# What a row gather of GpSimd waits for: its own view of the third last landing, or SyncE's count of the fourth last

## The chip, the cores and the metric

One Trainium2 chip (trn2), one of its NeuronCores. The metric is the device time of one execution in microseconds (us). The kernel before took 2842.06 us, the median of three runs (2833.11 to 2845.28).

## The reference

A relational graph layer and a mixture-of-experts layer, all float32, on N = 6250 nodes with 256 features.

```python
w_full = einsum('rb,bdo->rdo', w_comp, weight)        # 16 relations from 8 bases
msg = (feat @ w_full)[etypes, src] * norm             # 200,000 edges, sorted by dst
agg = segment_sum(msg, dst, num_segments=N)
x = x + relu(agg + h_bias + feat @ loop_weight)       # feat = layernorm(x)
# then: top 2 of 16 experts (256 -> 512 -> 256) for every node, added, and a layer norm
```

The targets `dst` are drawn as 6250·u² with u uniform, so low nodes have many edges and high nodes few. The host turns the order of the nodes round: the kernel begins with the nodes that have few edges.

## The kernel before, in words

The edges lie in 1568 blocks of 128. For each block GpSimd gathers the 128 source rows (1 KB each, 128 KB in all) from `feat` by an indirect DMA (line 1069) into `rows`, a ring of RB = 56 blocks. The nodes are cut into windows of 16. A step is one block with one window: VectorE builds the matrix `S` that spreads the block's edges over 16 nodes and 8 bases (lines 1141 to 1150), and TensorE multiplies it with the gathered rows into `psW` (line 1278, two passes of a float32 product). There are 1960 steps, 7 to a turn, 280 turns: each step moves on by a block or by a window, so a stretch of nodes with few edges has more steps to a block. After each 16 windows (a tile) ScalarE takes the sums out of `psW` (lines 1338, 1340), and TensorE transposes them and multiplies them with the basis weights (lines 1231, 1244).

What orders the gathers:

- **The lists.** `blocks(i)` of GpSimd issues 112 gathers in 8 groups of 14; there are 14 such passes, the first and the last written out with constants, those between in a loop whose waits take computed values. Before each group GpSimd waits until TensorE has finished the turns that read the ring's places (`s_P`, line 1059), and copies the next 14 columns of indices (line 1045).
- **The pacing.** Before each gather, `landed` (lines 1047 to 1050) waits for an earlier one: the gather of block j waits until that of block j - AHEAD has landed. A gather raises one of ROWS = 8 semaphores by 16 on landing, in turn, so GpSimd waits on that block's own semaphore. `ahead` (lines 719 to 722) does the same for the first 28 blocks, which are gathered at the end of the stage before (`expand`).
- **The count.** SyncE does little in this stage but wait for the landings one after the other, in order, and raise `s_in` by one for each (lines 1023 to 1026). TensorE waits on this one count before each turn (line 1275). Four times SyncE also waits for a turn of VectorE and loads the next coefficients (about 1 MB, lines 1032 and 1033). Before its first count it issues the loads of the layer's weights (lines 1018 to 1022).

When the graph layer ends, the experts' stage begins behind a barrier, then the last stage that adds up and normalizes.

Of the kernel before, what the change touches and what calls it, by code (L numbers as in the profile page):

```python
# [78 lines left out]
RB = 56  # L79
GB = 14  # L80
ROWS = 8
AHEAD = 3
IB = 2 * (RB // GB)
EG = 2
CTL_PART = (84, 72, 64, 60)
assert NBLK % RB == 0 and RB % GB == 0 and RB % ROWS == 0 and AHEAD < ROWS and sum(CTL_PART) == TURNS and all(n % NS == 0 for n in CTL_PART)
assert all(t + n <= 8 * i <= TURNS for t, n, i in CHUNK)
# [12 lines left out]
def at_least_one(e, loaded, held):  # L100

    for to, of in zip(held, loaded):
        e.reg_alu(to, of, 1, ALU.max)
    return held
# [74 lines left out]
def later(i):  # L179

    return not isinstance(i, int) or i > 0
# [468 lines left out]
def expand(nc, d, wcd, halfs, win_n, ident, tables, wend, pairs, jcol, wcol, spread, dstS, wgtS, coefS, s_got, s_feat, srcT, idx, rows, s_row):  # L650
# [5 lines left out]
    with ctx:  # L656
# [57 lines left out]
        def _(e):  # L714
# [4 lines left out]
            def ahead(j):  # L719
                if j >= AHEAD:  # L720
                    e.wait_ge(s_row[(j - AHEAD) % ROWS], 16 * ((j - AHEAD) // ROWS + 1))
                e.indirect_dma_start(rows[:, j * H:(j + 1) * H], None, d.feat, bass.IndirectOffsetOnAxis(ap=idx[:, j:j + 1], axis=0)).then_inc(s_row[j % ROWS], 16)
# [245 lines left out]
def graph_layer(nc, d, a, ctl, pairs, room, wend, srcT, dstS, wgtS, coefS, ident, wb, lw, hb, gw, s_w, logit, choice, mean, rstd, idx, rows, s_row):  # L968
# [5 lines left out]
    with ctx:  # L974
# [3 lines left out]
        def sem(name):  # L978
            return ctx.enter_context(nc.semaphore(name))
# [22 lines left out]
        s_in = sem("rows_in")  # L1002
# [10 lines left out]
        @blk.sync  # L1013
        def _(e):


            for c in range(HC):
                e.dma_start(wb[:, c, :, :], a["L0_gnn_weight"].rearrange("b (c p) o -> c p b o", p=P)[c, :, :, :]).then_inc(s_w, 16)
            e.dma_start(lw[:, :, :], a["L0_gnn_loop_weight"].rearrange("(c p) o -> p c o", p=P)).then_inc(s_w, 16)
            e.dma_start(hb[:, :], a["L0_gnn_h_bias"].partition_broadcast(P)).then_inc(s_w, 16)  # L1020
            e.dma_start(choice[0][:, :], a["L0_ffn_gate_b"].partition_broadcast(P)).then_inc(s_gb, 16)
            e.dma_start(gw[:, :, :], a["L0_ffn_gate_w"].rearrange("(c p) e -> p c e", p=P)).then_inc(s_w, 16)
            def rows_in(i):
                for j in range(RB):
                    e.wait_ge(s_row[j % ROWS], i * (RB // ROWS * 16) + (j // ROWS + 1) * 16)
                    e.sem_inc(s_in, 1)  # L1026
            i0 = 0
            for k, (t, n, i1) in enumerate(CHUNK):
                with e.Fori(i0, i1) as i:
                    rows_in(i)  # L1030
                e.wait_ge(s_S, t + n)
                c = slice(t * U * B, (t + n) * U * B)
                e.dma_start(coefS[:, c], d.coef[:, c]).then_inc(s_late[k], 16)
                i0 = i1
            with e.Fori(i0, NBLK // RB) as i:
                rows_in(i)

        @blk.gpsimd
        def _(e):
            ch = Chain(e, s_pool)  # L1040
            regs, room_held = ([e.alloc_register(f"{n}{q}") for q in range(IB)] for n in ("room", "room_held"))
            last = NBLK // (IB * GB) - 1

            def list_in(group, q):
                ch.add(e.tensor_copy(idx[:, q * GB:(q + 1) * GB], srcT[:, bass.ds(group * GB, GB)]))

            def landed(i, n):

                e.wait_ge(s_row[n % ROWS], i * (IB * GB // ROWS * 16) + (n // ROWS + 1) * 16)
                e.sem_inc(s_paced, 1)  # L1050

            def blocks(i):
                e.load(regs, room[0:1, bass.ds(i * IB, IB)])
                free = at_least_one(e, regs, room_held)
                for q in range(0 if later(i) else EG, IB):
                    if later(i) or q >= RB // GB:

                        e.wait_ge(s_P, free[q])
                        e.sem_inc(s_turn, 1)
                    if later(i) or q > EG:  # L1060
                        ch.wait()
                    if q < IB - 1 or not isinstance(i, int) or i < last:
                        list_in(i * IB + q + 1, (q + 1) % IB)
                    else:
                        e.sem_inc(s_turn, 1)
                    for u in range(GB):
                        at = (q * GB + u) % RB
                        landed(i, q * GB + u - AHEAD)
                        e.indirect_dma_start(rows[:, at * H:(at + 1) * H], None, d.feat, bass.IndirectOffsetOnAxis(ap=idx[:, q * GB + u:q * GB + u + 1], axis=0)).then_inc(s_row[at % ROWS], 16)  # L1069
            e.iota(choice[1][:, :], [[1, X]], base=-X, channel_multiplier=0, allow_small_or_imprecise_dtypes=True).then_inc(s_xno, 1)  # L1070
            e.iota(node.rearrange("p (m n) -> p m n", m=2), [[1, 2], [2, WIN // 2]], base=0, channel_multiplier=0, allow_small_or_imprecise_dtypes=True).then_inc(s_node, 1)
            blocks(0)
            with e.Fori(1, last) as i:
                ch.base, ch.n = IB * i - EG, 0
                blocks(i)
            ch.base, ch.n = IB * last - EG, 0
            blocks(last)
# [995 lines left out]
```

## Time and profile before

| | |
|---|---|
| median of 3 runs | 2842.06 us (2833.11 to 2845.28) |
| the profiled execution's own time, and its span | 2844.61 us, 2842.7 us |
| mean granted TensorE clock | 0.914 of full speed |
| busy: TensorE, VectorE, ScalarE, GpSimd | 78%, 34%, 23%, 64% |
| gathers of the graph layer (line 1069) | 1540, first start 159.5 us, last 2199.5 us |

The profile's page gives busy time by engine and line; the trace can be asked what an engine waited for before an instruction (its releaser), for a stretch of time, and for the instructions in order of time. In the rows "PE" is TensorE's matmuls, "POOL" GpSimd, "SPq" SyncE's queue; "x80" is a count; "us" of an idle time are summed over the count, and "issue" is idle time for which no releaser is seen. An indirect DMA's "busy" is the time in which GpSimd makes it, not its transfer.

### The profile page before, as it was taken

What the parts mean: (1) busy time and instruction counts of PE and PEld (TensorE: products, weight loads), DVE (VectorE), ACT (ScalarE), POOL (GpSimd) and SP (SyncE); (2) the same over time, 40 slices, a digit from 0 to 9 for tenths busy, and PEclk for the clock granted to TensorE, in tenths of its full rate; (3) what the DMA queues carried; (4) which work ended last, traced back from release to release, by engine and by line L of the source; (5) the groups of instructions that cost most, each with busy time, mean ns of one, the idle gap of its engine ahead of it and who ended that gap; (6) DMA issues with size and microseconds to landing.
All of it is one profiled execution on the core that took longest, in us unless ns stands there. A gap on an engine that the chain in (4) does not pass through costs nothing. (4 is left out here: it accounts for less than half of the span.)

```text
span 2842.7 us, 43421 instructions
## 1 busy us (share of the span) xinstructions
PE 2224.4 (78%) x11549; PEld 1849.9 (65%) x11550; DVE 967.4 (34%) x2172; ACT 654.3 (23%) x1539; POOL 1815.4 (64%) x2000
## 2 busy tenths in 40 slices
PE   1779999999988888876776768557655579999987
PEld 0567787877776666664664646445444379999975
DVE  6733333342332322222222212112112453333347
ACT  2522323232222211111110101001000233333345
POOL 0557777777777777777777777777777035555544
PEclk9999999999999989998898878789777799999998
DMA  6544444344333434334333333333333552222246
GB/s 210 160 146 119 121 118 123 116 120 134 116 117 111 129 111 116 111 112 122 109 109 109 118 107 108 108 100 114 103 103 94 187 182 70 70 70 70 70 131 220
DMA packets 146270, 338.66 MB, mean 119 GB/s; under 512 B 36674, under 2 KB 56290, under 8 KB 146051
## 3 DMA queue, kind: packets, MB, share of 16 engines
q0 software_dynamic: 89296, 245.33, 29.5%
q1 hardware_dynamic: 39311, 59.54, 6.1%
q10 hardware_dynamic: 17588, 32.88, 3.5%
q8 instruction: 36, 0.59, 0.1%
q14 instruction: 39, 0.32, 0.0%
HBM read 292.84 MB, written 47.97 MB: 120 GB/s over the span
## 5 line engine op out<-in xcount | busy, mean ns | idle before, releaser
L1069 POOL DMA_INDIRECT rows<-feat,idx x1540 | 1468.1, 953 | 548.9 <-issue 462.5
L1278 PE MATMUL psW<-rows,S 128*128 x3920 | 1065.1, 433 | 413.8 <-SPq L1026 380.8
L1278 PEld LDWEIGHTS psW<-rows,S 128*128 128x128 f32 x3920 | 842.1, 219 | 632.7 <-issue 495.0
L1150 DVE TENSOR_TENSOR S<-psHere,coefS 128x896 f32<-128x896 f32 x280 | 301.6, 1090 | 1379.0 <-PE psW L1278 1372.4
L1338 ACT COPY z<-psW 128x512 f32<-128x512 f32 x196 | 114.9, 586 | 1461.3 <-PE psW L1278 1460.6
L1244 PE MATMUL psG<-wb,zT 128*128 128x256 f32 (+1 forms) x1600 | 353.5, 379 | 0.0
L1244 PEld LDWEIGHTS psG<-wb,zT 128*128 128x128 f32 (+1 forms) x1600 | 300.6, 188 | 44.7
L1729 PE MATMUL psH<-xT,w1x 128*128 128x128 f32 x1840 | 226.8, 277 | 0.3
L1680 POOL DMA_INDIRECT expert_rows<-os,at_rows x114 | 114.0, 1000 | 171.3 <-DVE os L1788 171.3
L1729 PEld LDWEIGHTS psH<-xT,w1x 128*128 128x128 f32 x1840 | 216.5, 193 | 2.0 <-issue 1.9
L1738 PE MATMUL psO<-w2s,hT 128*128 x912 | 215.7, 379 | 0.0
L1702 ACT ACTIVATE hT<-psH,b1T 128x128 f32<-128x128 f32 x460 | 131.5, 368 | 315.6 <-PE psH L1729 315.6
L1676 POOL DMA_INDIRECT xs<-y_rows,at_rows x116 | 115.0, 991 | 100.7 <-POOLq L1408 56.6
L1738 PEld LDWEIGHTS psO<-w2s,hT 128*128 128x128 f32 x912 | 164.6, 190 | 17.6
L1788 DVE TENSOR_TENSOR os<-psO,b_b 128x256 f32<-128x256 f32 x114 | 48.4, 425 | 236.9 <-PE psO L1738 236.4
L1231 PE MATMUL psZ<-ident,z 128*128 128x128 f32 x784 | 113.8, 283 | 13.5 <-ACT zT L1352 8.8
L1340 ACT COPY psW<-zero 128x512 f32<-128x512 f32 x196 | 115.6, 590 | 6.2
L1352 ACT COPY zT<-psZ 128x512 f32<-128x512 f32 x196 | 108.1, 589 | 18.4 <-PE psZ L1231 18.4
L1231 PEld LDWEIGHTS psZ<-ident,z 128*128 128x128 f32 x784 | 83.7, 141 | 36.1 <-ACT zT L1352 20.1
L1772 DVE COPY w1x<-w1s 128x1024 f32 x116 | 86.1, 742 | 0.0
L1898 PE MATMUL psSum<-g,dg 128*128 128x256 f32 x200 | 56.0, 405 | 17.3 <-DMA g<-expert_rows 17.1
L1141 DVE TENSOR_TENSOR psHere<-dstS,psHere 128x224 f32<-128x224 f32 (+1 forms) x140 | 55.3, 395 | 31.5 <-DVE S L1150 25.1
(284 smaller groups left out, 1442.1 us busy)
## 6 DMA issues: line engine op xcount, KB each, us to landing
rows<-feat,idx POOLq DMA_INDIRECT x1568
g<-expert_rows SPq DMA_DIRECT2D x24, 512.0 KB, 5.5
w1s<-in_L_ffn_w SPq DMA_DIRECT2D x8, 1024.0 KB, 10.0
w2s<-in_L_ffn_w SPq DMA_DIRECT2D x16, 512.0 KB, 10.1
feat<-rows SPq DMA_DIRECT2D x24, 256.0 KB, 3.0
fts<-feat ACTq DMA_DIRECT2D x24, 256.0 KB, 2.8
h<-in_x ACTq DMA_DIRECT2D x24, 256.0 KB
y_rows<-y ACTq DMA_DIRECT2D x24, 256.0 KB
```

What stands on the lines that cost most here:

```text
L1069: e.indirect_dma_start(rows[:, at * H:(at + 1) * H], None, d.feat, bass.IndirectOffsetOnAxis(ap=idx[:, q * GB + u:q * GB + u + 1], axis=0) ...
L1150: e.tensor_tensor(S[h0 + h][:, :].rearrange("p (s b n) -> p s b n", s=U, b=B), both[:, h * U:(h + 1) * U, :].unsqueeze(2).to_broadcast([P, ...
L1231: last = e.transpose(to[:, k * P:(k + 1) * P], z[:, w * H + c * P:w * H + (c + 1) * P], ident[:, :])
L1244: last = e.matmul(psG[0:Q, m * H:(m + 1) * H], zT[:, at:at + Q], wb[:, c, b, :], start=False, stop=(c == HC - 1 and b == B - 1))
L1278: last = e.matmul(psW[:, bass.ds(bank[u], H)], S[h][:, u * ZC:(u + 1) * ZC], rows[:, bass.ds(slot[u], H)], start=False, stop=True, skip_gr ...
L1338: e.copy(z[:, 2 * k * H:2 * (k + 1) * H], bank).then_inc(s_z, 1)
L1340: e.copy(bank.rearrange("p (w o) -> p w o", w=2), zero[:, :].unsqueeze(1).to_broadcast([P, 2, H])).then_inc(s_clear, 1)
L1676: e.indirect_dma_start(xs[n % XS][:, :], None, d.y, bass.IndirectOffsetOnAxis(ap=at_rows[:, n, 0:1], axis=0)).then_inc(s_in[n % XS], 16)
L1680: e.indirect_dma_start(d.two, bass.IndirectOffsetOnAxis(ap=at_rows[:, n + 4, 1:2], axis=0), os_[n % 2][:, :], None).then_inc(s_out[n % 2], 16)
L1702: last = e.activation(hT[k][:, c * P:(c + 1) * P], psH[k][:, c * P:(c + 1) * P], ACT.Relu, bias=b1T[:, bass.ds(ex * FC + c, 1)])
L1729: last = e.matmul(psH[k][:, f * P:(f + 1) * P], w1x[k][:, c * F + f * P:c * F + (f + 1) * P], xT[k][:, c * P:(c + 1) * P], start=(c == 0), ...
L1738: last = e.matmul(psO[k][:, 0:H], hT[k][:, c * P:(c + 1) * P], w2s[:, bass.ds(ex, 1), c, :].rearrange("p e f -> p (e f)"), start=(c == 0), ...
```

## The change

Two places differ. `landed` waits on `s_in`, the count that SyncE keeps, and no longer on the semaphore of the block's own gather; and AHEAD is 4, in `landed` and in `ahead`.

```diff
@@ -79,7 +79,7 @@
 ROWS = 8
-AHEAD = 3
+AHEAD = 4
 IB = 2 * (RB // GB)
@@ -1046,7 +1046,7 @@
             def landed(i, n):
 
-                e.wait_ge(s_row[n % ROWS], i * (IB * GB // ROWS * 16) + (n // ROWS + 1) * 16)
+                e.wait_ge(s_in, i * (IB * GB) + (n + 1))
                 e.sem_inc(s_paced, 1)
```

In the order of GpSimd's instructions this shows in the loop of `blocks`. First the head of the loop, a group's first gathers, before (line 1059's wait is named turn_done, line 1026's count rows_in):

```order
 L1045 COPY idx<-srcT 128x14
 L1049 REGISTER_ALU
 L1069 DMA rows<-feat,idx 128x256 [waits row5]
 L1069 DMA rows<-feat,idx 128x256 [waits row6]
 L1069 DMA rows<-feat,idx 128x256 [waits row7]
 L1049 REGISTER_ALU
 L1069 DMA rows<-feat,idx 128x256 [waits row0]
```

The same place with the change:

```order
 L1045 COPY idx<-srcT 128x14
 L1049 REGISTER_ALU
 L1069 DMA rows<-feat,idx 128x256 [waits rows_in]
 L1049 REGISTER_ALU
 L1069 DMA rows<-feat,idx 128x256 [waits rows_in]
 L1049 REGISTER_ALU
 L1069 DMA rows<-feat,idx 128x256 [waits rows_in]
```

The value waited for differs for every gather now, so nearly every one has a register operation ahead of it: 110 to a pass of the loop against 15, where 8 gathers shared one value. No other engine's instructions move.

## Rows read from the trace of the kernel before

**Rows 1.** The page: busy by line; line, engine, operation | busy, mean ns | idle before, releaser
```profile
L1069 POOL DMA_INDIRECT rows<-feat,idx x1540 | 1468.1, 953 | 548.9 <-issue 462.5
L1278 PE MATMUL psW<-rows,S 128*128 x3920 | 1065.1, 433 | 413.8 <-SPq L1026 380.8
```
**Rows 2.** Waits of the whole span: who waited for whom: us in total, times, longest us
```profile
POOL rows L1069 <- issue: 462.5, 1422, 3.4
PE psW L1278 <- SPq L1026: 380.8, 132, 7.8
POOL rows L1069 <- DMA rows<-feat,idx: 85.6, 116, 4.6
```
**Rows 3.** GpSimd in order of time, 1471 to 1486 us: start, us, what [idle before]
```profile
1469.73 1.48 POOL L1069 DMA_INDIRECT rows<-feat,idx  x1 [0.64 <-DMA rows<-feat,idx]
1471.52 0.95 POOL L1069 DMA_INDIRECT rows<-feat,idx  x1 [0.30 <-issue]
1472.77 0.95 POOL L1069 DMA_INDIRECT rows<-feat,idx  x1 [0.30 <-issue]
1474.02 0.95 POOL L1069 DMA_INDIRECT rows<-feat,idx  x1 [0.30 <-issue]
1475.27 0.98 POOL L1069 DMA_INDIRECT rows<-feat,idx  x1 [0.30 <-issue]
...
1482.81 0.94 POOL L1069 DMA_INDIRECT rows<-feat,idx  x1 [0.30 <-issue]
1484.06 0.94 POOL L1069 DMA_INDIRECT rows<-feat,idx  x1 [0.30 <-issue]
```
**Rows 4.** The stage's end, 2195 to 2210 us, in order of time
```profile
2199.46 0.95 POOL L1069 DMA_INDIRECT rows<-feat,idx  x1 [0.89 <-DMA rows<-feat,idx]
2203.64 4.97 PE L1278 MATMUL psW<-rows,S 128*128 x14 [2.50 <-SPq L1026]
```
**Rows 5.** Waits, 560 to 2200 us
```profile
POOL rows L1069 <- issue: 377.6, 1160, 3.4
PE psW L1278 <- SPq L1026: 369.8, 121, 7.8
POOL rows L1069 <- DMA rows<-feat,idx: 58.7, 80, 3.3
```
**Rows 6.** GpSimd at the longest waits for a landing, one near each load of coefficients
```profile
655.61 0.95 POOL L1069 DMA_INDIRECT rows<-feat,idx  x1 [3.30 <-DMA rows<-feat,idx]
954.81 0.95 POOL L1069 DMA_INDIRECT rows<-feat,idx  x1 [2.96 <-DMA rows<-feat,idx]
1328.10 0.94 POOL L1069 DMA_INDIRECT rows<-feat,idx  x1 [2.28 <-DMA rows<-feat,idx]
1622.62 0.94 POOL L1069 DMA_INDIRECT rows<-feat,idx  x1 [1.91 <-DMA rows<-feat,idx]
```
**Rows 7.** GpSimd, 311 to 316 us: one of 14 long waits without a releaser
```profile
311.68 0.98 POOL L1069 DMA_INDIRECT rows<-feat,idx  x1 [0.16 <-issue]
315.28 0.95 POOL L1069 DMA_INDIRECT rows<-feat,idx  x1 [2.62 <-issue]
```
**Rows 8.** The stage's start: GpSimd's gathers, SyncE's loads and first count
```profile
159.49 1.00 POOL L1069 DMA_INDIRECT rows<-feat,idx  x1 [0.57 <-issue]
167.61 0.95 POOL L1069 DMA_INDIRECT rows<-feat,idx  x1 [4.61 <-DMA rows<-feat,idx]
163.46 0.49 SPq L1022 DMA_DIRECT2D gw<-in_L_ffn_gate_w  x1
L1026 SPq EVENT_SEMAPHORE  x1568: 17/17/17, 164.2 to 2203.3; - x196
```
**Rows 9.** Busy by stretch: us, PE busy (x), PEld, DVE, ACT, POOL, clock, DMA, GB/s
```profile
260.00:360.00 100.00, 93.71 (x462) 78.49 (x460) 33.19 (x79) 31.06 (x56) 71.67 (x81) 1.00 0.40 119
560.00:2200.00 1640.00, 1219.88 (x4995) 981.77 (x4994) 432.69 (x873) 243.16 (x438) 1201.11 (x1329) 0.88 0.38 112
```
**Rows 10.** Waits, 360 to 560 us
```profile
POOL rows L1069 <- DMA rows<-feat,idx: 8.4, 15, 1.2
PE psW L1278 <- SPq L1026: 1.4, 4, 0.6
```
**Rows 11.** All engines at 367 to 369 us: a turn's end and the list behind it
```profile
367.88 1.09 DVE L1150 TENSOR_TENSOR S<-psHere,coefS 128x896 f32<-128x896 f32 x1 [25.68 <-PE psW L1278]
368.33 0.21 POOL L1045 COPY idx<-srcT 128x14 int32 x1
```
**Rows 12.** Line 1049, GpSimd's register operations: ns min/median/max, first and last start
```profile
L1049 POOLq ALU_OP  x180: 32/32/39, 273.8 to 2045.4; - x180
```

## The prediction

> **What bounds the kernel now.** I read the costliest lines first, then who waited for whom, then the same by stretch of time, and last the gathers one by one. The gathers run from 159.5 to 2199.5 us, 72% of the time, and in that stage TensorE stands idle 380.8 us for SyncE's count of landed rows [rows 1, 2]. SyncE is only a messenger there: it counts what lands. So the question is what sets the pace of the gathers. One by one they stand 1.25 us apart, 0.953 us of making in the mean [rows 1] and a gap of 0.30 us without a releaser [rows 3]. That is GpSimd's own pace: 1539 steps at 1.253 us would take 1928 us, and the stage's gathers take 2040 us. Of the 112 us between, the view of waits puts 85.6 us of idle time, over 116 gathers, down to the landing of an earlier gather [rows 2]; each of those would have had its gap of 0.30 us anyway, so 85.6 - 116 × 0.30 = 51 us are real. The end of the stage is tied to the last gather: it starts at 2199.46, TensorE's last turn waits for it until 2203.64, and all that follows stands behind [rows 4]. What GpSimd saves all along therefore comes off the end, unless TensorE is the bound in some part.
>
> **What the change does to a landing wait.** With three gathers in flight, the fourth starts without delay if the first has landed within 3 × 1.25 - 0.30 = 3.46 us of its start. Most do: 1422 of 1540 show no such wait [rows 2]. With four in flight the limit is 4.71 us. A wait of x us of idle time now leaves max(0, x - 0.30 - 1.25).
>
> The stage is not the same throughout, so I take it in three parts.
>
> *From 560 us on.* TensorE is idle 369.8 us for rows [rows 5] and busy 1220 of 1640 us [rows 9]; it follows GpSimd. Landing waits: 58.7 - 80 × 0.30 = 34.7 us. Four are longer than the new limit hides, each near a load of coefficients [rows 6]: they keep 1.75 + 1.41 + 0.73 + 0.36 = 4.2 us, which leaves 30.5. Some waits for landings must be among those without a releaser. Those hold 377.6 - 1160 × 0.30 = 29.6 us above the gap; 12 waits like that of rows 7, some 2.4 us each above the gap, make 28.5 of it; but the 89 gathers behind a list copy have a gap of only 0.16 us, as the first of [rows 7], which saves 12.5, so about 14 us are of another kind. The heads of GpSimd's loop are in it too; I take 4 us as landings. Together 34.5 us.
>
> *Before 360 us.* TensorE is busy 93.7 of 100 us [rows 9], at the full clock: nodes with few edges have many steps to a block, and TensorE is the bound. At 368.33 GpSimd copies a list as soon as the turn that frees the ring has ended (VectorE, which waited for TensorE too, starts at 367.88) [rows 11]. There the ring is full, and what GpSimd saved by then it waits for TensorE instead. I take nothing.
>
> *360 to 560 us.* Landing waits are worth 8.4 - 15 × 0.30 = 3.9 us, but TensorE waited for rows only 1.4 us in all [rows 10]. I take 1 us, between nothing and 3.9.
>
> **What it adds.** (1) At the start, the first gather now needs SyncE's count of 25, and SyncE issues weight loads until 163.95 and first counts at 164.2; before, that gather started at 159.49 [rows 8]. It will start about 5 us or more later, at 165 to 168. But the fourth gather started at 167.61 in any case, so what is lost at the fourth is 1 to 4 us; it lies in the part where TensorE is the bound, and costs nothing. (2) SyncE stands between landing and gather. One count takes 17 ns [rows 8], and the relay is a few hundredths of a microsecond out of 1.25 us of new room; where SyncE is held (four coefficient loads) the gathers could be held with it, which I put at no more than 1 us each. (3) Register operations: 110 - 15 = 95 more in each of 12 passes of the loop, 1140 in all, 32 ns each [rows 12]. GpSimd's queue runs them while the last gather is being made: of the gathers of [rows 3], the first, the fourth and the last have such an operation ahead of them now (places 0, 3 and 11 of the group), and the gaps of the fourth and the last are 0.30 us like those between. I put this at nothing; if the cover is gone it is 1140 × 0.032 = 36 us. (4) The 14 long waits of [rows 7] come one in 106 gathers, whatever the list: the next gather starts 3.60 us after the last, a time in which that last one can just have landed. This looks like a wait until nothing is in flight. It doesn't depend on AHEAD, and I leave it. (5) The 28 gathers of `expand` end before a barrier that others are late for: nothing.
>
> **The sum** is 34.5 + 0 + 1 = 35.5 us off the profiled execution's 2844.6, which gives 2809. That execution lies 2.5 us above the median of the runs shown; off the median it is 2842.1 - 35.5 = **2807 us**. The bounds: nothing at one end; at the other all landing waits, 51 us and some 6 among those without a releaser, 2842 - 57 = 2785.
>
> Against this stands a price. A gather of 128 KB that starts clean should have landed long before the third next in the trace; most gaps of 0.30 us say that it does [rows 3]. The Trainium skill, "DMA: Bandwidth & Descriptors", section "Anatomy of one DMA — SWDGE (gpsimd) path", gives a DMA of this path about 2.0 us plus its bytes over 436 GB/s, by which I estimate 2.3 us for 128 KB. By that rule alone three in flight are enough, no gather ever waits, and the sum would be nothing: 2842. The trace disagrees in 116 places of 1540 [rows 2]: these are late landings, and the page's figure has no spread.
>
> **The rivals.** Faster is over 0.5% (14 us) off, about what a measurement of this kernel can tell from no change.
>
> *A. The lateness moves along (0.13).* If gathers are late because the transfers before them in the same queues are, a fourth in flight is only later still, and each wait comes back at 1.25 us more. For it: the long waits come with 1 MB loads [rows 6], and the page's rule would also end here. Against it: after each wait the following gathers run at once at 1.25 us, and the 16 DMA engines are at 0.38 to 0.40 of their time [rows 9]. Result: 0 to 14 us off, 2828 to 2842.
>
> *B. TensorE takes back more (0.08).* The ring could also be full at places past 560 us once GpSimd is earlier. TensorE's waits for rows are 369.8 us there, so it has room on the whole; if it holds GpSimd until about 900 us, a third of the landing waits go to it: 20 to 25 us off, 2820.
>
> *C. Slower (0.07).* The added register operation lies in GpSimd's gap, not under its making. At 32 ns each the gain is just used up (36 us); with the wait on one semaphore that changes each time it could be 0.07 us, 1140 × 0.07 = 80 us, and the result 2807 + 80 = 2887. The point from which it decides is 0.031 us a gather. Against it: the equal gaps of [rows 3].
>
> *D.* That the change does nothing (the wait never binding before) is excluded by the 116 waits.
>
> **How the numbers follow.** The forecast has 0.72, A 0.13, B 0.08, C 0.07. Faster by over 0.5% is the forecast and B: 0.80; within 0.5%: A, 0.13; slower: C, 0.07. The range for 8 in 10 goes from 2790, somewhat inside of the bound of 2785, over B to 2832, some way into A; it leaves out C and most of A.
>
> **What the profile after would show.** The gathers' steps stay at 1.25 us, with 0.95 busy and a gap of 0.30: a gap of 0.33 or more is C. Waits of the gathers put down to SyncE's count or a landing shrink from 85.6 us of idle time to below 20; if they stay above 50, it is A. Waits for TensorE before gathers or list copies appear between 160 and 560 us, some 5 to 10 us; if they go on past 600 us, B. The last gather starts near 2164, not 2199.5. TensorE's wait for SyncE's count falls by about what the stage gets shorter, from 380.8 to some 345. The stages behind keep their length. I am wrong if the last gather starts after 2185, or if time is lost or won behind it.

## The result and the profile after

The changed kernel took 2809.5 us in the median of four runs (2809.2 to 2812.0), against 2843.5 for the kernel before in the same comparison: a ratio of 0.9888, with a 95% interval of 0.9867 to 0.991. It is 34 us faster, where 35.5 were forecast. Its profiled execution has a span of 2807.4 us.

The lines of the page that answer to [rows 1]: the gathers' idle time is 57 us less, TensorE's 35 us less.

```profile
L1069 POOL DMA_INDIRECT rows<-feat,idx x1540 | 1464.3, 951 | 492.0 <-issue 432.2
L1278 PE MATMUL psW<-rows,S 128*128 x3920 | 1065.6, 434 | 379.0 <-SPq L1026 347.0
...
q14 instruction: 94, 0.77, 0.1%
```

The last line is new to the argument: the DMA queue that brings instructions moved 94 packets. In the kernel before it moved 39:

```profile
q14 instruction: 39, 0.32, 0.0%
```

Who waited for whom, over the whole span, answering to [rows 2] (us in total, times, longest): waits of gathers now name SyncE's count, and there are waits of list copies for TensorE (the third row).

```profile
PE psW L1278 <- SPq L1026: 347.0, 126, 6.7
POOL rows L1069 <- SPq L1026: 58.3, 94, 7.1
POOL idx L1045 <- PE psW L1278: 14.8, 5, 6.9
```

The stage's end, answering to [rows 4]. The last gather starts at 2162.84, 36.6 us earlier; behind it lie 644.6 us of the span, before 643.2. The change acts in this stage alone.

```profile
2162.84 0.95 POOL L1069 DMA_INDIRECT rows<-feat,idx  x1 [0.30 <-issue]
2168.56 4.97 PE L1278 MATMUL psW<-rows,S 128*128 x14 [2.63 <-SPq L1026]
```

**Where the 36.6 us come from.** GpSimd's timeline gives the start of each gather. From each start I take the start before it and GpSimd's own step of 1.253 us; what is left over is sorted by the place. A *head* is the first gather of a pass of the loop (blocks 112, 224, ..., 13 of them); a *stall* is one of the 14 places 106 gathers apart (blocks 141, 247, ...); *ring full* is a group's first gather, no head, whose list copy waited for the turn of TensorE that frees its places (blocks 182 and 252); *late landings* are all others more than 0.03 us over the step, without those behind a list copy. In us over 1.253 a gather:

| | before | after |
|---|---|---|
| first gather of this stage starts at | 159.5 | 165.2 |
| blocks 29 to 55 | 7.4 | 0.4 |
| late landings | 53.9 | 12.3 |
| 14 stalls | 33.1 | 17.4 |
| 13 heads | 8.9 | 25.3 |
| ring full | 0 | 9.3 |

The differences are +5.7 - 7.0 - 41.6 - 15.7 + 16.4 + 9.3 = -32.9; list copies and GpSimd's plain steps, 0.003 us shorter, give the other 3.7. Two of the rows that moved most were not in my sum, and they cancel.

**A stall.** GpSimd, 304 to 309 us of the changed kernel, the same place as [rows 7]; the gather that started 3.60 us after the one ahead of it now starts 2.28 us after.

```profile
306.41 0.98 POOL L1069 DMA_INDIRECT rows<-feat,idx  x1 [0.16 <-issue]
308.69 0.94 POOL L1069 DMA_INDIRECT rows<-feat,idx  x1 [1.30 <-SPq L1026]
```

Line 1050 runs in GpSimd's queue right behind each gather's wait, so its times tell when that wait was passed (line, queue, operation, count: ns, first and last start). First the changed kernel, then the kernel before:

```profile
L1050 POOLq EVENT_SEMAPHORE  x2: 17/17/17, 305.3 to 308.5; - x2
```

```profile
L1050 POOLq EVENT_SEMAPHORE  x2: 17/17/17, 311.9 to 315.1; - x2
```

In both, GpSimd's queue has passed the gather's wait and takes 3.2 us until the next wait is passed; the gather starts 3.4 us after its wait was passed (308.69 - 305.3, 315.28 - 311.9). The stall is therefore a pause in the queue that hands instructions on, of the same length in both. It is no wait for a landing. What differs is how far the queue was ahead of the making of the gathers: with one more gather allowed in flight, it passed the wait 1.1 us before the gather ahead started, not 0.2 us after it.

**A head.** GpSimd at 419 to 424 us (block 224), changed kernel, then the kernel before:

```profile
419.63 0.95 POOL L1069 DMA_INDIRECT rows<-feat,idx  x1 [0.30 <-issue]
422.22 0.20 POOL L1045 COPY idx<-srcT 128x14 int32 x1 [1.64 <-issue]
423.10 0.98 POOL L1069 DMA_INDIRECT rows<-feat,idx  x1 [0.68 <-SPq L1026]
```

```profile
421.96 0.94 POOL L1069 DMA_INDIRECT rows<-feat,idx  x1 [0.30 <-issue]
423.10 0.21 POOL L1045 COPY idx<-srcT 128x14 int32 x1 [0.20 <-issue]
423.94 0.98 POOL L1069 DMA_INDIRECT rows<-feat,idx  x1 [0.63 <-DMA rows<-feat,idx]
```

The loop's own instructions at that place show a gap between the branch back and the first operation behind it. Changed kernel, then before:

```profile
L1073 POOLq COMPARE_BRANCH  x1: 53/53/53, 418.1 to 418.1; - x1
L1073 POOLq FUSED_REGOPS  x1: 73/73/73, 421.0 to 421.0; - x1
```

```profile
L1073 POOLq COMPARE_BRANCH  x1: 53/53/53, 421.6 to 421.6; - x1
L1073 POOLq FUSED_REGOPS  x1: 68/68/68, 421.9 to 421.9; - x1
```

2.9 us against 0.3. And two packets of the instruction queue moved just there, from 419 to 424.5 us of the changed kernel, where the same stretch before (420 to 424.5 us) has none:

```profile
q14 instruction: 2, 0.02, 0.7%
```

So the branch's target was no longer at hand and was fetched. The body now executes 367 instructions a pass instead of 271 (counted in the trace between two heads). The loop turns back 11 times; the 55 more packets are five of 8 KB for each. The first and the last of the 13 heads have no branch back before them, and cost 0.06 us each.

**Ring full.** GpSimd at 359 to 368 us of the changed kernel, the place of [rows 11]: it stands 6.9 us for TensorE's turn.

```profile
359.02 0.95 POOL L1069 DMA_INDIRECT rows<-feat,idx  x1 [0.30 <-issue]
366.88 0.19 POOL L1045 COPY idx<-srcT 128x14 int32 x1 [6.92 <-PE psW L1278]
```

### The profile page after: what moved, and what is told of

Same layout as the page of the kernel before. It is cut to its first block and busy times, and to the rows that moved or that the text cites. A ratio compares the mean times of both kernels' runs of the same rounds, so it can differ in the third digit from the quotient of the medians.

```text
span 2807.4 us, 44573 instructions
## 1 busy us (share of the span) xinstructions
PE 2223.8 (79%) x11549; PEld 1851.5 (66%) x11550; DVE 965.7 (34%) x2172; ACT 653.3 (23%) x1539; POOL 1810.5 (64%) x2000
## 5 line engine op out<-in xcount | busy, mean ns | idle before, releaser
L1231 PE MATMUL psZ<-ident,z 128*128 128x128 f32 x784 | 113.7, 283 | 13.5 <-ACT zT L1352 8.8
L1898 PE MATMUL psSum<-g,dg 128*128 128x256 f32 x200 | 55.8, 404 | 17.3 <-DMA g<-expert_rows 17.2
```

The costliest lines, as they stand in the source:

```text
L1231: last = e.transpose(to[:, k * P:(k + 1) * P], z[:, w * H + c * P:w * H + (c + 1) * P], ident[:, :])
```

## The experiments

Theory: the deeper flight hides late landings and lengthens the lead of GpSimd's queue, which hides its pauses; the new form of the wait costs nothing in itself, but makes the loop's body longer, so that it is fetched again at each turn back. The rivals: the heads come from the deeper flight, or from the waits on a computed count; the stalls wait for landings; and the prediction's A, that more gathers in flight land later.

The measured values come first, in us, all sorted as above. Times are medians of four runs beside the kernel before (2840.1 to 2844.0 us in these comparisons). "Own semaphores" is the wait of the kernel before, "count" that of the change; "4 ahead" is AHEAD = 4.

| kernel | time | ratio to before, 95% | late | stalls | heads | ring full | fetch packets | last gather |
|---|---|---|---|---|---|---|---|---|
| own semaphores, 4 ahead | 2790.5 | 0.9832 (0.9815 to 0.9848) | 12.3 | 16.3 | 7.6 | 12.5 | 40 | 2141.0 |
| count, 3 ahead | 2877.3 | 1.0131 (1.0114 to 1.0148) | 53.4 | 34.0 | 39.2 | 0 | 94 | 2229.4 |
| own, 4 ahead, again | 2791.3 | 0.9829 (0.9812 to 0.9845) | 13.4 | 15.3 | 7.1 | 12.7 | 39 | 2143.7 |
| own, 4 ahead, 98 more raises a pass | 2808.5 | 0.9875 (0.9859 to 0.9892) | 11.9 | 18.3 | 27.2 | 10.5 | 95 | 2162.1 |
| count, 4 ahead, passes of 56 | 2789.3 | 0.9827 (0.981 to 0.9843) | 13.0 | 17.6 | 4.2 | 11.2 | 36 | 2144.1 |
| own, 5 ahead | 2775.5 | 0.9771 (0.9754 to 0.9787) | 7.9 | 2.8 | 11.4 | 14.5 | 39 | 2128.7 |
| count, 5 ahead | 2784.2 | 0.9792 (0.9775 to 0.9809) | 8.1 | 1.4 | 16.7 | 13.5 | 94 | 2135.5 |
| own, 7 ahead | 2771.8 | 0.9752 (0.9735 to 0.9768) | 6.3 | 0.0 | 13.0 | 14.5 | 39 | 2124.1 |

Two heads (blocks 112 and 448) can themselves be waits with a full ring: on own semaphores they are 5.2 of the 7.6 us with four ahead, 10.0 of the 11.4 with five and 12.3 of the 13.0 with seven; on the count with five ahead block 448 is 3.8 of the 16.7. The other heads without a fetch then cost 0.06 us each in the median.

**A first job with another bound.** Four kernels ran first beside a kernel before that itself took 3667.9 us.

```diff
-AHEAD = 3
+AHEAD = 4
```

This is the first of them, own semaphores with four ahead; the edits of the second and the third are shown below, and the fourth has AHEAD = 5.

> Alone the half of the change that lets four gathers be in flight: AHEAD = 4, but GpSimd still waits on each gather's own semaphore. The loop keeps its 15 register operations. Theory 'longer loop': the gain of the deeper flight comes in full (late landings about 42 us, the stalls one in 106 gathers about 16 us), less some 9 us given back to TensorE where the ring is full, and the heads of the loop keep 0.7 us each over a plain step instead of 1.9. Last gather near 2146, time about 2793 us, 16 us below the change. Rival 'the deeper flight itself makes the loop's heads dearer': as the change, about 2810 us, heads at 1.9 us.

> Alone the other half: GpSimd waits for SyncE's count, but of the third last block (AHEAD = 3). Theory 'longer loop': the 13 heads of the loop cost 1.9 instead of 0.7 us over a plain step, 16 us more; late landings and the stalls one in 106 stay as before, the relay by SyncE adds 0 to 5 us. Time 2859 to 2865 us: slower than before. Rival 'the relay is free and the loop's length too': 2843 us.

> AHEAD = 4 on the gathers' own semaphores, with a register operation whose result nobody reads ahead of most gathers in the loop, as many as the change has, and no wait on SyncE's count. Theory 'longer loop' (the loop's instructions no longer stay where GpSimd reads them, and are fetched again at each turn back): heads at 1.9 us over a plain step, instruction fetches near 94 instead of 39 packets, time 16 us above the kernel with own semaphores alone, 2809 us. Rival 'the wait on one count does it, not the length': heads at 0.7 us, 2793 us.

> AHEAD = 5 on own semaphores. One gather in 106 takes GpSimd's queue 3.1 us to hand over instead of 0.5. Theory 'lead': this is a fixed time, of which as much is hidden as the queue is ahead of the making of the gathers; one more in flight gives up to 1.25 us more lead, and the 14 stalls sink from 1.2 to between 0 and 0.3 us over a plain step: 13 to 17 us less than with four, 2778 us where TensorE takes none of it back, 2784 where it does. Rival 'the stall waits for a landing': with five in flight the stall stays at 1.2 us or grows again, 2790 us or more.

Measured: 3742.2 us (ratio 1.0172, 1.0119 to 1.0225), 3648.0 (0.9956, 0.9915 to 0.9996), 3747.0 (1.0194, 1.0139 to 1.0249) and 3731.4 (1.0145, 1.0096 to 1.0194). None of the expectations came true or could be judged, since GpSimd was not the bound: in the first kernel it stood 764 us for TensorE before its list copies, while its own steps and the stages behind kept their lengths, and TensorE showed 568 us of idle time without a releaser (17 us in the usual profile of the kernel before).

```profile
POOL idx L1045 <- PE psW L1278: 764.4, 31, 36.5
PE psW L1278 <- issue: 567.6, 298, 14.3
```

What held TensorE there stays open. These four ran on another chip than all the kernels below; whether it was the chip isn't shown. In that job, where GpSimd waited for TensorE, the deeper flight gained nothing and lost 1.5 to 1.9%. All that follows is from jobs in which the kernel before took its usual time.

**The deeper flight alone**, the first kernel again:

> The same kernel as the first (AHEAD = 4 on the gathers' own semaphores), again, since in the first job the kernel before itself took 3668 us and TensorE, not GpSimd, was the bound. If the kernel before is back at 2843 us: theory 'longer loop' 2793 us, rival 'the deeper flight makes the heads dearer' 2810 us. If it stays at 3668 us, TensorE's own waits have the say, and this kernel again takes some 2% more than the kernel before.

2790.5 us, 19 us below the change. The heads are at 0.6 us each in the mean, there are 40 fetch packets, and stalls and late landings are as in the change. The deeper flight does not make the heads dearer.

**The count alone:**

```diff
-                e.wait_ge(s_row[n % ROWS], i * (IB * GB // ROWS * 16) + (n // ROWS + 1) * 16)
+                e.wait_ge(s_in, i * (IB * GB) + (n + 1))
```

> The second kernel again (the count alone, AHEAD = 3), beside a kernel before that should take its 2843 us. Theory 'longer loop': heads of the loop at 1.9 us over a plain step, time 2859 to 2865 us, slower than before by 16 to 22 us. Rival 'relay and loop length are free': 2843 us.

2877.3 us: slower by 36 us, with the right sign and cause, but more than the 16 to 22 expected. Late landings (53.4) and stalls (34.0) are as before (53.9 and 33.1), so the relay by SyncE costs less than this sorting can see; two profiles of one kernel differ by 1.1 us in late landings. The heads cost 39.2 us, 3.0 each and not 1.9: with three ahead the queue has less lead to cover the fetch. The first gather starts at 164.4, 4.9 us later.

**Is it the length?**

```diff
-AHEAD = 3
+AHEAD = 4
...
+            spare = e.alloc_register("spare")
...
                         landed(i, q * GB + u - AHEAD)
+                        if not isinstance(i, int) and (q * GB + u) % ROWS:
+                            e.reg_alu(spare, regs[0], u, ALU.max)
```

> The third kernel again (AHEAD = 4, own semaphores, an unread register operation ahead of most gathers of the loop). Own semaphores alone took 2790.5 us. Theory 'longer loop': 13 heads 1.2 us dearer, 2806 us, instruction fetches near 94 packets. Rival 'it is the wait on the count': 2790 us, heads at 0.7 us, 39 packets.

2791.3 us, which looks like the rival; but the trace shows that the added operations were never in the program: 43,421 instructions, as in the kernel without them. The build left the unread register operation out. The run is a repetition of own semaphores with four ahead (2790.5 and 2791.3), and says nothing on the length. In its place, also with AHEAD = 4:

```diff
+                        if not isinstance(i, int) and (q * GB + u) % ROWS:
+                            e.sem_inc(s_paced, 1)
```

> AHEAD = 4 on own semaphores, and in the loop passes 98 more semaphore raises that nobody waits for (e.sem_inc of s_paced ahead of 7 gathers in 8): about as many more instructions in the body as the change has register operations, and neither register operations nor the count. It stands in for the third kernel, whose unread register operations were not among its instructions (its loop is that of the first). Theory 'longer loop': fetches near 94 packets, heads of the loop 1.2 us or more dearer, 2806 to 2812 us against 2790.5. Rival 'it is the computed values or the wait on the count, not the length': 2791 us, heads as with own semaphores, 39 packets.

2808.5 us, 44,597 instructions, 95 fetches, heads of 2.1 us. Neither a computed value for each gather nor the count is in this kernel. Together with the next one it leaves the length: the length makes the heads.

**Half the body**, on the changed kernel:

```diff
-IB = 2 * (RB // GB)
+IB = RB // GB
```

> The change with passes of 56 gathers instead of 112 (IB = 4): the loop's body is half as long, its heads are 27 instead of 13. Theory 'longer loop': half the body needs no new fetch, each head costs 0.7 us over a plain step, 27 × 0.7 = 19 against 25 us now: 2803 us, fetches near 39 packets. Rival 'a head costs 1.9 us whatever the body's length' : 27 × 1.9 = 52 us, 2836 us.

2789.3 us, 14 us better than expected: 36 fetch packets, and all 27 heads cost 5.0 us together, 2.5 of them at block 448, where GpSimd waits for TensorE; the others are at 0.06 us in the median. The 0.7 a head of the expectation was the price with three ahead. A head of a body that needs no fetch is covered with four. This kernel keeps the count and the computed values and is as fast as own semaphores with four ahead: apart from the length, the form of the wait costs nothing.

**The lead**, with AHEAD = 5 on own semaphores and on the count, and 7 on own semaphores:

> The fourth kernel again (AHEAD = 5, own semaphores), against 2790.5 us with four. Theory 'lead': the 14 stalls, 3.1 us in GpSimd's queue each, sink from 1.2 us over a plain step to 0 to 0.3: 2774 to 2783 us. Rival 'the stall waits for a landing': it stays at 1.2 us or grows, 2786 us or more.

> The change with AHEAD = 5 (SyncE's count of the fifth last block). Theory 'lead': a pause of GpSimd's queue costs its length less the lead, whether it is the long hand-over one in 106 (1.2 us left with four, 0.2 with five) or the fetch at the loop's head (3.0 us over a plain step with three, 1.9 with four): with five the heads fall to some 0.9 us, the stalls to 0.2: 13 × 1.0 + 14 × 1.0 = 27 us off 2809.5, 2780 to 2786 us. Rival 'the heads' cost is fixed': 25 us in heads stay, only stalls and late landings go, 2791 to 2795 us.

> AHEAD = 7 on own semaphores, the most that eight semaphores allow. Five took 2775.5 us, with 2.8 us left in the 14 stalls, 8 in late landings, 11 in heads and 15 where GpSimd waits for TensorE. Theory 'lead': the lead is limited by how many gathers GpSimd's queue can hand over ahead, so what is left of late landings goes (8 us) and little else: 2764 to 2774 us. Rival 'more in flight crowds the transfers': landings get later for all, TensorE's rows come later, 2776 us or more.

2775.5, 2784.2 and 2771.8 us, each in its range; only the late landings, which seven ahead was to remove, fell from 7.9 to 6.3 us and no further. The 14 stalls fall from 33.1 us (three ahead) over 15 to 18 (four) to 2.8 and 1.4 (five) and 0.0 (seven); the heads with fetch from 39.2 over 25.3 to 16.7. Their medians fit one rule. The *lead* here is the time from line 1050, when the queue has passed a gather's wait, to that gather's start, the median of the 1540; "turn back" is the median of the 11 heads behind a branch back; all in us:

| kernel | lead | a stall | lead + stall | a turn back | lead + turn back |
|---|---|---|---|---|---|
| count, 3 ahead | 0.97 | 2.37 | 3.34 | 3.49 | 4.46 |
| count, 4 ahead (the change) | 2.21 | 1.12 | 3.33 | 2.24 | 4.45 |
| count, 5 ahead | 3.45 | 0.00 | | 0.96 | 4.41 |
| own, 7 ahead | 6.00 | 0.00 | | 0.06 | |

The pause has one length in all of them, and what shows of it is the length less the lead. With seven ahead, GpSimd at the place of the stall runs through:

```profile
305.11 0.98 POOL L1069 DMA_INDIRECT rows<-feat,idx  x1 [0.16 <-issue]
306.39 0.95 POOL L1069 DMA_INDIRECT rows<-feat,idx  x1 [0.30 <-issue]
```

The rivals (a wait for a landing; a fixed cost of a head) fall. What is left with seven ahead is 1539 × 1.253 = 1928 us of GpSimd's own steps, of 1967 between its first and last gather. It is the fastest by its median, 72 us below the kernel before and 38 below the change; its interval overlaps that of own semaphores with five ahead.

**Do more gathers in flight land later?** The traces tell without another run. From a gather's start to SyncE's count of it pass 2.77 us in the median in the kernel before, in the change and with seven ahead, and 2.85, 2.86 and 2.87 us in the mean (blocks 60 and later); the prediction's estimate was 2.3. Of these 1508 gathers 78 took longer than 3.46 us before, the limit with three in flight. After the change 86 did, but the limit was 4.71 us then, and 10 were longer than that. So rival A falls: the landings stayed as they were, and the limit moved past most of the late ones.

## Why the prediction was right, point by point

The time (2807 forecast, 2809.5 measured), the place (the gathers of this stage; last gather forecast near 2164, measured 2162.8) and the mechanism that the sum rests on, late landings under a wider limit, were right. Two terms put at nothing were not.

- **Late landings from 560 us on**, 34.5 us: measured 31.0 (42.0 before, 11.0 after, blocks 330 and later). The room of one step was taken rightly, but the waits beside the coefficient loads keep more than the 1.75 and 1.41 us I left them (2.70 and 1.83 above the gap); here the first two of [rows 6] after the change:

```profile
650.77 0.95 POOL L1069 DMA_INDIRECT rows<-feat,idx  x1 [3.00 <-SPq L1026]
941.59 0.95 POOL L1069 DMA_INDIRECT rows<-feat,idx  x1 [2.13 <-SPq L1026]
```

- **Before 560 us**, 1 us: late landings fell by 10.6 us, and 9.3 us came back with the ring full, at the very list copy that the forecast named, and once more about 100 us later. TensorE as the bound of that part was read rightly. A little of rival B is there too: with four ahead on own semaphores, and half a body, the ring is full at block 448, 712 us, for 2.5 us; in the change that place falls together with a fetch.
- **The start**, no cost: the first gather came 5.7 us later (5 or more forecast), the next 27 blocks lost 7.0 us less.
- **The relay**: nothing measurable (late landings 53.9 with own semaphores, 53.4 with the count).
- **Register operations**, term (3), nothing: right in that they lie under the making (the gaps stayed 0.30 us; 1152 more in the trace, 1140 forecast), wrong in what it left out. I priced the operations and not the room they take. The longer body is fetched at each turn back: 16.4 us. The Trainium skill, "Runtime: NRT & Kernel Launch", section "Instruction fetch mechanics", says that a taken branch whose target is not in the window of instructions at hand must wait for a fetch of it. The trace agrees in the kind: 2.9 us from branch to target against 0.3. It gives the window of engines other than TensorE as 32 KiB, 512 instructions, in two blocks of 256. By count alone both 271 and 367 would fit; how these bodies lie across the blocks no run here shows. Here 367 to 369 were fetched anew and 271 were not, and the measurement decides.
- **The stalls**, term (4), left as they were: wrong. From one row I read "a wait until nothing is in flight", as a landing was just possible in the step of 3.60 us. It was a pause of fixed length in the queue, and one more gather in flight hid 15.7 us of it. The waits of line 1050 beside the gather's start, both in the trace before, would have told: the queue had passed the wait 3.3 us before the gather started.

So 31 of my 34.5 us were where I put them, but that the time came out within 3 us is luck: two terms that I had at nothing were -15.7 and +16.4, and either alone would have moved the result by nearly half of the gain. The list of what the profile would show had no row on either, which is why they could hide.

One sign on that list spoke against me as I wrote it. Waits of gathers put down to SyncE's count or a landing were to shrink from 85.6 to below 20 us, and above 50 was to mean rival A; they are 58.3. But the view names SyncE now where it named nothing before: 17.2 us of them are stalls, 7.1 the first gather, 4.1 heads. The 68 waits elsewhere in a group, from block 56 on, hold 27.4 us, 7 above their gaps, where 97 held 69.4 before, 40 above theirs. The sign should have been counted above the gap and place by place.

Another sign, waits of list copies for TensorE past 600 us, was to mean rival B. There are three, at 716, 1009 and 1444 us, 6.5 us in all. All three are heads behind a fetch, and GpSimd's queue passed the wait for TensorE there without standing at it.

## What to carry to other kernels

Count how far an engine's queue runs ahead of the engine: a pause in the queue (a long hand-over, a fetch at a branch) costs only what exceeds that lead, so a pacing wait that is one place looser can pay at places that have nothing to do with what it waits for. Here the lead was 1.0, 2.2, 3.5 and 6.0 us with three, four, five and seven ahead, and the pauses 3.3 and 4.4. When an edit adds instructions to a loop, look at the length of the body as well as at the time of each, and at the packets of the instruction queue. And if a wait only limits how many transfers are in flight, raise the limit first and leave the form of the wait: that alone was worth 50 us here with four and 72 with seven, in the jobs where the gathers were the bound.

## What the runs showed of the hardware that was not expected

- One gather in 106 took GpSimd's queue 3.1 to 3.5 us to hand on, in every kernel of the table at the same places (blocks 141, 247, ...), whatever its lists and passes; at block 671 the loop's turn back falls into the same time. What the queue does in it isn't shown.
- A body of 367 to 369 executed instructions was fetched again at each turn back (94 or 95 packets in all, five of 8 KB for each of 11 turns back), one of 271 was not (39 or 40), nor one of 186 (36).
- A semaphore count relayed through SyncE cost GpSimd's waits nothing that can be seen: late landings were 53.4 us with it and 53.9 without, three ahead.
- Up to seven gathers in flight hardly made each other later: from start to count 2.77 us in the median with three and with seven, 2.85 and 2.87 in the mean.
- In one job the same kernel before took 3668 us; GpSimd waited for TensorE in the kernels profiled there, and why TensorE stood stays open.
